# First loads and first weights of a two-layer feed-forward and attention kernel: x rows on two queues, factors applied at the transposed rows, w0 in quarters, w1 by ScalarE and GpSimd row by row

## What is computed

```python
def ffn(x, k0, k1, k2, s0, s1, s2):           # k0 512x1024, k1 1024x1024, k2 1024x256, bool
    dense = lambda k, h: h @ where(k, 1.0, -1.0)
    h = s0 * dense(k0, concatenate([x, -x], -1))
    h = s1 * dense(k1, relu(h) * 2)
    return s2 * dense(k2, relu(h) * 2)

x = x + 0.5 * ffn(layernorm(x), ...)
x = x + attention(layernorm(x), wq, bq, wk, bk, wv, bv, wo, bo)   # 16 heads of 16
x = x + 0.5 * ffn(layernorm(x), ...)
```

## Time and profile before

| | us |
|---|---|
| median of 3 runs | 1539.21 (1538.98 to 1539.43) |
| the profiled execution | 1539.0 |
| its span in the trace | 1535.1 |
| TensorE busy | 1512.7 (99% of the span) |
| ScalarE busy | 1130.6 (74%) |
| VectorE busy | 585.1 (38%) |
| GpSimd busy | 59.7 (4%) |
| TensorE's share of the chain that ended last | 97% |

### The profile page before, as it was taken

One profiled execution on the slowest core, in us unless ns is written; L12 is line 12 of the kernel. 1 busy time (PEld: TensorE's weight loads), 2 busy tenths in 40 slices (PEclk: granted clock), 3 DMA queues, 4 the chain that ended last, 5 costly groups with the idle time before them and its releaser, 6 DMA issues.

```text
span 1535.1 us, 31520 instructions
## 1 busy us (share of the span) xinstructions
PE 1512.7 (99%) x12441; PEld 599.4 (39%) x12441; DVE 585.1 (38%) x1329; ACT 1130.6 (74%) x1647; POOL 59.7 (4%) x65
## 2 busy tenths in 40 slices
PE   6999999999999999999999999999999999999999
PEld 3555455334333333433333333333334334333354
DVE  6556755511531252325332242332322323332272
ACT  3221221888898888888989888988988988998711
POOL 2010111000000010010010000000000000000000
PEclk9999999999999999999999999999999999999999
DMA  4221323312231331223212113112212211311110
GB/s 124 55 83 35 88 70 105 87 40 73 74 67 53 103 102 43 55 95 94 80 50 81 55 39 107 39 40 67 80 39 67 80 39 53 100 49 37 36 42 16
DMA packets 110516, 101.44 MB, mean 66 GB/s; under 512 B 56225, under 2 KB 95905, under 8 KB 110369
## 3 DMA queue, kind: packets, MB, share of 16 engines
q1 hardware_dynamic: 109392, 98.86, 22.7%
q10 hardware_dynamic: 976, 0.53, 0.1%
HBM read 61.87 MB, written 25.43 MB: 57 GB/s over the span
## 4 chain that ended last, share of the span: by engine, by line
PE 97%; DVE 1%; POOL 0%; DMA 0%; issue 0%; ACT 0%; SPq 0%; POOLq 0%; DVEq 0%
PE psum L804 31%; PE psum L768 29%; PE psum L788 16%; PE psum L671 12%; PE psum L683 3%; PE psum L659 3%; PE psum L690 2%; PE psum L704 1%; PE psum L697 0%; POOL square L1072 0%; DMA x_sb<-in_x 0%; DVE h_lo L904 0%; DVE xn L995 0%; DVE square L1052 0%; PE psum L647 0%
## 5 line engine op out<-in xcount | busy, mean ns | idle before, releaser
L860 ACT ACTIVATE prob<-psum 128x512 f32<-128x512 f32 (+1 forms) x1432 | 1018.3, 787 | 127.4 <-PE psum L788 121.4
L804 PE MATMUL psum<-prob,v_sb 128*17 128x512 f32 x4096 | 490.0, 595 | 0.0
L788 PE MATMUL psum<-q_st,k_st 64*128 64x512 f16 x2048 | 350.0, 379 | 2.7 <-DVE flag L1059 1.3
L833 ACT ACTIVATE h_hi<-psum 128x512 f16<-128x512 f32 x183 | 109.8, 605 | 216.4 <-PE psum L671 161.1
L902 DVE TENSOR_SCALAR h_hi<-psum 128x512 f16<-128x512 f32 x73 | 50.5, 692 | 434.4 <-PE psum L768 434.4
L904 DVE SCALAR_TENSOR_TENSOR h_lo<-psum,h_hi 128x512 f16<-128x512 f32 x256 | 168.5, 687 | 81.1 <-ACT h_hi L833 78.7
L804 PEld LDWEIGHTS psum<-prob,v_sb 128*17 128x17 f32 x4096 | 96.4, 96 | 261.4 <-issue 165.2
L788 PEld LDWEIGHTS psum<-q_st,k_st 64*128 64x128 f16 x2048 | 82.1, 94 | 280.8 <-ACT prob L860 209.1
L768 PE MATMUL psum<-h_hi,w 64*128 64x512 f16 x1184 | 151.9, 376 | 0.3 <-DVE h_lo L904 0.3
L768 PE MATMUL psum<-h_lo,w 64*128 64x512 f16 x1184 | 151.8, 376 | 0.0
L671 PE MATMUL psum<-h_hi,w 128*128 128x512 f16 x432 | 102.1, 379 | 0.0
(11 more groups left out here) (101 smaller groups left out, 871.7 us busy)
## 6 DMA issues: line engine op xcount, KB each, us to landing
k_st<-k_halves SPq DMA_DIRECT2D x64, 512.0 KB, 4.4
q_halves<-piece SPq DMA_DIRECT2D x32, 256.0 KB, 2.5
q_st<-q_halves SPq DMA_DIRECT2D x64, 128.0 KB, 4.9
x_rows<-x_sb SPq DMA_DIRECT2D x16, 256.0 KB, 2.2
k_halves<-piece SPq DMA_DIRECT2D x16, 256.0 KB, 2.9
att_rows<-o_sb SPq DMA_DIRECT2D x128, 32.0 KB
x_sb<-x_rows SPq DMA_DIRECT2D x8, 512.0 KB, 4.4
att_t<-att_rows SPq DMA_DIRECT2D x16, 256.0 KB
```

The costliest lines, as they stand in the source:

```text
L788: mm = pe.matmul(psum[:, score_bank[h + r], :], k_st[rows, slot, t * P:(t + 1) * P], q_st[rows, slot, :], start=True, stop=True)
L804: mm = pe.matmul(psum[32 * j:32 * j + va, O_BANK, :], v_sb[:, b * key_tiles + t, GROUP * g4 + j, :], prob[:, h % PROBS, :], start=(t == 0) ...
L833: act.activation(hi, psum[:, bank, :], ACT.Relu).then_inc(act_done, 1)
L860: act.activation(prob[:, to:to + count, :], psum[:, bank:bank + count, :], ACT.Exp, scale=score_scale / QK_SCALE ** 2).then_inc(exp_sem, 1)
```

## The change

- The four tiles of block 0 are issued by two queues, tiles 0 and 2 by SP and 1 and 3 by ACT, ahead of everything else. ACT's scales and `k0` stand behind its two tiles. On SP `k1` follows its two tiles, and block 1 of x is issued behind all weights.
- The norm of block 0 is no longer multiplied by `scal[:, 12]` (L975 multiplies by 1.0 there). Instead the two f16 parts of the transposed rows are: ACT's copy takes the factor as its scale, and DVE's subtraction becomes a multiply and subtract. Both now wait for `scal_done`; DVE's norm doesn't.
- TensorE's first four transposes each wait for their own tile of `xn` and no longer for all four.
- w0 is made in four quarters of 256 columns, the first ahead of the first `lo` part of `xt`, the second between the two, the rest behind. `l1` waits for a quarter at banks 0, 2, 4 and 6.
- w1: the even rows stay with ACT, but one row stands before each even bank of `l1` and not all four before bank 0. The odd rows go from DVE to POOL, which does them, four instructions, ahead of w2.

```diff
--- before.py
+++ after.py
@@ -53,7 +53,7 @@
 
 
 FILLS = {
-    "turn_x": (4, (1, 1), (0, 2)),
+    "turn_x": (4, (1, 1), (1, 1)),
     "l1": (4, (1, 1), (0, 2)),
     "l2": (16, (1, 1), (0, 2)),
     "l3": (32, (0, 1), (0, 1)),
@@ -190,8 +190,10 @@
             steps += [Step("l1", ahead, m) for m in range(2, kh)]
         return steps + [Step("load", u + RING - 1)]
 
-    side = norm_turn(0, 0) + [Step("w0", 0, 0)] + turns("turn_x", 0) + [Step("w0", 0, 1), Step("w1")]
-    side += [Step("l1", 0, m) for m in range(kh)]
+    side = norm_turn(0, 0) + [Step("w0", 0, 0), Step("turn_x", 0, 0), Step("w0", 0, 1), Step("turn_x", 0, 1)]
+    side += [Step("w0", 0, 2), Step("w0", 0, 3)]
+    for m in range(kh):
+        side += [Step("w1", 0, m), Step("l1", 0, m)]
     for u in range(2 * blocks):
         side += layers(u, u + 1 if u + 1 < 2 * blocks else None, u - 1 if 0 < u <= blocks + 1 else None)
     side = [s for s in side if s.kind != "load" or s.u < 2 * blocks]
@@ -476,8 +478,8 @@
 
         consts, scal_done, table_seed, table_ready = (
             sem(n) for n in ("consts", "scal_done", "table_seed", "table_ready"))
-        w0_done, w1_act, w1_dve, w2_done, qk_scaled = (
-            sem(n) for n in ("w0_done", "w1_act", "w1_dve", "w2_done", "qk_scaled"))
+        w0_done, w1_act, w1_pool, w2_done, qk_scaled = (
+            sem(n) for n in ("w0_done", "w1_act", "w1_pool", "w2_done", "qk_scaled"))
 
         mm_done, act_done, dve_done = sem("mm_done"), sem("act_done"), sem("dve_done")
         ln, ln_x, split, flipped, merged, squared, peaked, bo_added, halves = (
@@ -526,7 +528,12 @@
             ts = slice(i * tpb, (i + 1) * tpb)
             sp.dma_start(x_sb[:, u % RING], (x_tiles if u < blocks else x1_tiles)[:, ts, :]).then_inc(x_in[u % RING], 16)
 
+        def load_x0(queue, t):
+            queue.dma_start(x_sb[:, 0, t, :], x_tiles[:, t, :]).then_inc(x0_in[t], 16)
+
         def act_loads():
+            for t in range(1, tpb, 2):
+                load_x0(act, t)
             for n, s in enumerate((s0, s1, s2)):
                 act.dma_start(scal[:, n:n + 1], s.broadcast_to((P, 1))).then_inc(scal_in, 16)
             for k in range(kd):
@@ -534,10 +541,9 @@
                               ).then_inc(k0_in[k], 16)
 
         def sp_loads():
-            for t in range(tpb):
-                sp.dma_start(x_sb[:, 0, t, :], x_tiles[:, t, :]).then_inc(x0_in[t], 16)
+            for t in range(0, tpb, 2):
+                load_x0(sp, t)
             sp.dma_start(k1_raw, k1.rearrange("(k p) n -> p k n", p=P)).then_inc(k1_in, 16)
-            load_x(1)
             sp.dma_start(k2_raw, k2.rearrange("(k p) n -> p k n", p=P)).then_inc(k2_in, 16)
             for dst, src in ((wq_sb, wq), (wk_sb, wk), (wv_sb, wv), (wo_sb, wo_t)):
                 sp.dma_start(dst[:], src.rearrange("(k p) n -> p k n", p=P)).then_inc(weights_in, 16)
@@ -547,7 +553,7 @@
                                  ).then_inc(weights_in, 16)
             sp.dma_start(bv_sb[:], bv.rearrange("h a e -> a (h e)").broadcast_to((P, dim))).then_inc(weights_in, 16)
             sp.dma_start(bo_sb[:], bo.rearrange("(a n) -> a n", a=1).broadcast_to((P, dim))).then_inc(weights_in, 16)
-            for u in range(2, RING - 1):
+            for u in range(1, RING - 1):
                 load_x(u)
 
         def pool_constants():
@@ -564,6 +570,10 @@
                                pattern=[[hd, hpt], [0, hd // 4]], channel_multiplier=-1).then_inc(consts, 1)
             pool.memset(v_sb[:, :, :, hd:va], 1.0).then_inc(consts, 1)
             pool_scalars()
+            pool.wait_ge(k1_in, 16)
+            for k in W1_POOL:
+                pool.tensor_scalar(w1[:, k, :], k1_raw[:, k, :], scal[:, 13:14], scal[:, 14:15], ALU.mult, ALU.add
+                                   ).then_inc(w1_pool, 1)
             pool.wait_ge(k2_in, 16)
             pool.tensor_scalar(w2[:], k2_raw, 2.0, -1.0, ALU.mult, ALU.add).then_inc(w2_done, 1)
             pool.wait_ge(weights_in, WEIGHTS_IN)
@@ -592,24 +602,21 @@
 
         def dve_w0(m):
 
-            cols = slice(m * hidden // 2, (m + 1) * hidden // 2)
+
+            cols = slice(m * hidden // 4, (m + 1) * hidden // 4)
             for k in range(kd):
                 dve.wait_ge(k0_in[k], 16)
                 dve.tensor_tensor(w0[:, k, cols], k0_raw[:, k, cols], k0_raw[:, kd + k, cols], ALU.subtract
                                   ).then_inc(w0_done, 1)
 
-        def dve_w1():
-            dve.wait_ge(k1_in, 16)
-            for k in range(1, kh, 2):
-                dve.tensor_scalar(w1[:, k, :], k1_raw[:, k, :], scal[:, 13:14], scal[:, 14:15], ALU.mult, ALU.add
-                                  ).then_inc(w1_dve, 1)
-
-        def act_w1():
+
+        W1_ACT, W1_POOL = range(0, kh, 2), range(1, kh, 2)
+
+        def act_w1(k):
             act.wait_ge(k1_in, 16)
             act.wait_ge(scal_done, SCALARS)
-            for k in range(0, kh, 2):
-                act.activation(w1[:, k, :], k1_raw[:, k, :], ACT.Identity, scale=scal[:, 13:14], bias=scal[:, 14:15]
-                               ).then_inc(w1_act, 1)
+            act.activation(w1[:, k, :], k1_raw[:, k, :], ACT.Identity, scale=scal[:, 13:14], bias=scal[:, 14:15]
+                           ).then_inc(w1_act, 1)
 
 
 
@@ -641,8 +648,9 @@
                     pe.wait_ge(exp_sem, s.free_exp)
             for j in range(s.lo, s.hi):
                 if s.kind == "turn_x":
+                    if m == 0:
+                        pe.wait_ge(ln_x, j + 1)
                     if j == 0 and m == 0:
-                        pe.wait_ge(ln_x, tpb)
                         pe.wait_ge(consts, IDENT)
                     mm = pe.transpose(psum[:, bank, j * P:(j + 1) * P], xn[:, 0, j, m * P:(m + 1) * P], ident[:])
                 elif s.kind == "l1":
@@ -652,8 +660,8 @@
                     if u == 0 and m == 0 and half == 0:
                         wait_hi(pe, find["turn_x", u, k])
                         pe.wait_ge(w0_done, k + 1)
-                    if u == 0 and m == kh // 2 and j < kd:
-                        pe.wait_ge(w0_done, kd + k + 1)
+                    if u == 0 and m in (2, 4, 6) and j < kd:
+                        pe.wait_ge(w0_done, kd * m // 2 + k + 1)
                     if u == 0 and m == 0 and half == 1:
                         pe.wait_ge(dve_done, find["turn_x", u, k].dve)
                     mm = pe.matmul(psum[:, bank, :], w0[:, k, m * P:(m + 1) * P], xt[:, half, k, :],
@@ -662,10 +670,10 @@
                     half, k = divmod(j, kh)
                     if m == 0 and half == 0:
                         wait_hi(pe, find["l1", u, k])
-                        if u == 0 and k % 2 == 0:
-                            pe.wait_ge(w1_act, k // 2 + 1)
-                        if u == 0 and k % 2 == 1:
-                            pe.wait_ge(w1_dve, k // 2 + 1)
+                        if u == 0 and k in W1_ACT:
+                            pe.wait_ge(w1_act, W1_ACT.index(k) + 1)
+                        if u == 0 and k in W1_POOL:
+                            pe.wait_ge(w1_pool, W1_POOL.index(k) + 1)
                     if m == 0 and half == 1:
                         pe.wait_ge(dve_done, find["l1", u, k].dve)
                     mm = pe.matmul(psum[:, bank, :], w1[:, k, m * P:(m + 1) * P], (h0_hi, h0_lo)[half][:, k, :],
@@ -821,12 +829,14 @@
                 if s.kind == "score":
                     act_exps(s.u, (0, 4, 6)[s.m], (4, 6, 8)[s.m])
                 elif s.kind == "w1":
-                    act_w1()
+                    if m in W1_ACT:
+                        act_w1(m)
                 elif not s.on_act or s.kind not in FILLS or not s.last():
                     continue
                 elif s.kind == "turn_x":
                     act.wait_ge(mm_done, s.mm)
-                    act.activation(xt[:, 0, m, :], psum[:, bank, :], ACT.Copy).then_inc(act_done, 1)
+                    act.wait_ge(scal_done, SCALARS)
+                    act.activation(xt[:, 0, m, :], psum[:, bank, :], ACT.Copy, scale=scal[:, 12:13]).then_inc(act_done, 1)
                 elif s.kind in ("l1", "l2"):
                     hi = (h0_hi if s.kind == "l1" else h1_hi)[:, m, :]
                     act.wait_ge(mm_done, s.mm)
@@ -881,18 +891,13 @@
                     dve_peak()
                 elif s.kind == "w0":
                     dve_w0(m)
-                elif s.kind == "w1":
-                    dve_w1()
                 elif s.kind not in FILLS or not s.last():
                     continue
                 elif s.kind == "turn_x":
-                    if s.on_act:
-                        dve.wait_ge(act_done, s.act)
-                    else:
-                        dve.wait_ge(mm_done, s.mm)
-                        dve.tensor_copy(xt[:, 0, m, :], psum[:, bank, :]).then_inc(dve_done, 1)
-                        dve.wait_ge(dve_done, s.hi_dve)
```

(11 more changed lines are left out.)

## The result

| | before | with the change |
|---|---|---|
| median | 1539.30 us | 1541.88 us |
| the profiled execution | 1539.0 | 1541.06 |
| its span | 1535.1 | 1537.1 |
| start of `l2` in the chain | 22.91 | 25.28 |
| start of `l3` of block 0 in the chain | 50.54 | 53.00 |

Over 22 runs with the change and 21 before, the ratio is 1.0017, with a 95% interval from 1.0011 to 1.0023: the change makes the kernel 2.6 us slower. (A twenty-second run before, of 2076.41 us at a low clock, is in the median of the table and not in the ratio.) I had forecast 1537.1, in a range from 1535.9 to 1539.4. The sign is wrong and the time lies outside the range; that it stays within 0.2% held.

What follows compares the result with a forecast made beforehand. TensorE, busy 99% of the span, was taken to bound the kernel, so only `l2`'s earlier start counts. 2.9 + 0 - 0.5 - 0.3 = 2.1 us earlier gave 1536.9, median 1537.1, range 1535.9 to 1539.4.

Steps and rivals of the forecast that it cites:

- Term 1: Block 0's x tiles on two queues: the fourth tile's statistics start at 5.1; gain 2.9 us, bounds zero to 3.0.
- The rival that only issue time is won: Loading x: the fourth tile still takes 5.8 and lands at 7.05; gain 0.2 us, 1539.0; chance 0.18.
- Term 5: Remaining loads: third scale lands at 7.3, `k0` at 8.9 and 9.9, in time; booked 0, bound 1 us.
- term 4: POOL's four rows of w1 slow DVE's second quarter of w0; loss 0.3 us, bounds 0 to 0.6.
- The rival on the slow side: `k0`'s issue held behind SP's backlog, second part landing at 16.0; 1541.7 us; chance 0.10 together with a slow POOL row.
- TensorE's speed: Start of `l1`: the change from 1.2 to 2.4 GHz may come later; booked 0, bound 0.9 us.
- Term 3: ACT alternates w1 rows with `l1` evictions, so TensorE stalls in `l2`'s first bank; loss 0.5 us, bounds 0.3 to 0.9.
- Term 2: Transposing by tile wins 0.6 us, spent by the w0 quarter before the second `lo` part; sum 0, possibly 0.4 gain.
- DVE idle before w0 on a DMA of `prob`: Sign of a wrong forecast, before w0: DVE waits for a load, pointing to `k0` held behind SP's backlog.
- matmuls of `l1` at the low level behind bank 1: Sign of a wrong forecast, in `l1`: a matmul of 609 ns behind bank 1.

Runs made afterwards that it cites:

- k1_behind_k0: The changed kernel, but SP waits for both parts of `k0` to land before it issues `k1`; 1536.95 us, ratio to before 0.9984.
- scales_first: The changed kernel, but ACT issues the three scales ahead of its two tiles of x; 1548.56 us, ratio to before 1.0059.

## Why the prediction was wrong, step by step

**Term 1, the rows of x: right, and too small.** I took 2.9 with 3.0 as the upper bound; the normed tiles came 3.36 earlier. The first tile itself landed sooner (DVE starts at 3.62, not at 4.00). The rival that only issue time is won is refuted for the rows: all four landed in 2.6 to 3.1 after their issue. But the scales and `k0` lost more than x won.

**Term 5, the queues: the step that failed.** I carried 4.7 for the third scale and 5.8 to 6.3 for `k0` over from the earlier trace rows and booked zero, with 0.8 and 0.5 of cover. They took 7.8, 9.6 and 10.2. The latencies of the earlier trace rows are not properties of these transfers but of their place: before, the scales and the first part of `k0` were issued ahead of `k1`, at 0.79 to 2.20, and `k1` at 2.71. With the change `k1` is issued at 1.74, beside the first scale. I had written that `k0` "now shares the engines with a `k1` issued ahead of it" and gave it no price. A row of the kernel before already showed it: the 256 KB of k2, issued behind `k1`, were 10.6 us under way. The second part of `k0` landed at 13.85 where 9.9 was taken, and the fourth matmul of `l1` started at 16.91. With `k1` held back (k1_behind_k0) it starts at 12.95, so the step cost 3.96 us there, the 0.55 of term 4 included (POOL's rows come later in that run), and turned a gain of 3.35 into a loss of 0.61. In that run the slower `l1` takes back 1.04 and the interleaving 0.32, and the marker ends 2.00 ahead of before. That this is so near the 2.1 of the forecast is partly luck: more was won on x than I took, and the clock level, booked at zero, took it back.

**The rival on the slow side had the right consequence and the wrong cause.** I gave `k0` held behind SP's backlog 0.10 together with a slow row of POOL, with 1541.7 as its time. The measured 1541.88 is close to it partly by chance. `k0` was issued nearly on time (3.15 to 5.10, against 3.15 to 4.13 with `k1` held back) and not after 10.2; it was late between issue and landing. It landed at 13.85, 2.2 earlier than that rival said, and the clock level made up for most of that. By the rival's own threshold, a landing at 13.6, 13.85 would have cost 0.25 and not 2.6. That SP's queue was full, no run shows; the traces show that its issue of wq took 5.40.

**TensorE's speed: mis-sized.** Booked zero, bound 0.9 on the ground that behind bank 1 ACT sets the pace. Measured: 1.75. TensorE had three matmuls to do in six microseconds, until the last needed `lo` part, and then ran nine 0.43 apart, into bank 2. ACT didn't hide it: it waited for TensorE, 1.11 before its second eviction. Nor do the bounds add up as the prediction states them: 2.9 less 0.9, 0.6 and 1.0 leaves 0.4, which is 1538.8 and not 1538.4, and with the 0.9 of TensorE 1539.7, outside the range.

**Term 4, POOL beside DVE: mis-sized.** I took 0.3. With the change the second operation of the first quarter took 0.63 instead of 0.42 and the second quarter 1.09 where it takes 0.75 with POOL idle: 0.55 on the path. The lock as worked out would have allowed 1.9. POOL's rows were dearer too, 5.97 for four and not 3.8 to 4.6, where they took 4.74 in scales_first beside DVE's short operations; TensorE never waited for them.

**Term 3, the interleaving: right where it can be seen.** 0.5 was booked; it is 0.11 with the change, hidden by the slow `l1`, 0.32 in k1_behind_k0, and 0.48 once `l1` is fast.

**Term 2: right.** The earlier transposes brought nothing by themselves, and the quarter of w0 between the `lo` parts is on the path. Behind `l2` nothing changed, as said; block 1 behind all weights cost nothing. Of the signs that I had named, DVE idle before w0 on a DMA of `prob`, and matmuls of `l1` at the low level behind bank 1, are both in the trace.
